# Hybrid block on one core: the tail's order, side work of the attention loop, and the choice of experts from logits

## What is computed

```python
x = x + attn_a(layernorm(x), ...)
x = x + ffn(layernorm(x), Wr, W1, b1, W2, b2)
x = x + attn_b(layernorm(x), ...)
x = x + ffn(layernorm(x), Wr, W1, b1, W2, b2)

def attn_a(x):      # groups of 32 tokens: squared relu attention in the group, and a linear state over earlier groups
    o = (v_quad + v_lin) * gate
    return o @ Wout + bout

def attn_b(x):      # 16 heads of 64; the softmax is over the queries
    scores = einsum('bhqp,bhkp->bhqk', q, k) / sqrt(64)
    ctx = einsum('bhqk,bhkp->bqhp', softmax(scores, axis=2), v)
    return ctx.reshape(b, s, 1024) @ l_w.T + l_b

def ffn(x):         # 8 experts, two for each token, room for 160 tokens an expert and batch
    probs = softmax(x @ Wr); topk_probs, topk_experts = top_k(probs, 2)
    keep = pos < capacity       # pos: place of the token among those of its expert, in order
    h = relu(buf @ W1 + b1); y = h @ W2 + b2
    return (y[of the token's slot] * keep * topk_probs).sum(over the two)
```

## Time and profile before

| | us |
|---|---|
| median of 3 executions (1459.59 to 1462.47) | 1459.8 |
| the profiled execution | 1459.8 |
| its span, first to last instruction | 1458.1 |
| TensorE busy | 1422.4 (98%) |
| VectorE busy | 1071.0 (73%) |
| ScalarE busy | 917.9 (63%) |
| GpSimd busy | 279.9 (19%) |

### The profile page before, as it was taken

One profiled execution on the slowest core, in us unless ns is written; L12 is line 12 of the kernel. 1 busy time (PEld: TensorE's weight loads), 2 busy tenths in 40 slices (PEclk: granted clock), 3 DMA queues, 4 the chain that ended last, 5 costly groups with the idle time before them and its releaser, 6 DMA issues.

```text
span 1458.1 us, 43372 instructions
## 1 busy us (share of the span) xinstructions
PE 1422.4 (98%) x18426; PEld 1016.6 (70%) x18426; DVE 1071.0 (73%) x2172; ACT 917.9 (63%) x1727; POOL 279.9 (19%) x325
## 2 busy tenths in 40 slices
PE   7999989999999999999999999999999999999997
PEld 6989954656777665657777756577777567777487
DVE  6885058898677678886666788876667887787764
ACT  5775756666666666666666666666666666666544
POOL 5165713022210012120000121400000213000046
PEclk9999999999999999999999999999999999999999
DMA  8501311012110111010000110110101111101002
GB/s 224 204 19 56 93 44 43 16 27 53 26 26 17 35 29 31 25 45 17 16 16 17 43 32 22 36 33 17 31 16 40 31 26 33 35 17 31 2 19 59
DMA packets 44464, 58.30 MB, mean 40 GB/s; under 512 B 8231, under 2 KB 32656, under 8 KB 44144
## 3 DMA queue, kind: packets, MB, share of 16 engines
q1 hardware_dynamic: 35120, 38.27, 9.5%
q0 software_dynamic: 9152, 17.26, 4.4%
HBM read 22.14 MB, written 19.32 MB: 28 GB/s over the span
## 4 chain that ended last, share of the span: by engine, by line
PE 87%; DVE 6%; issue 3%; POOL 2%; ACT 2%; DMA 1%; POOLq 0%; DVEq 0%; ACTq 0%
PE bank L1153 30%; PE bank L1166 29%; PE bank L1076 6%; PE bank L1081 4%; PE bank L1090 3%; PE bank L1308 2%; PE bank L1304 2%; PE bank L412 1%; PE bank L1265 1%; PE bank L446 1%; DVE stats L1349 1%; PE bank L830 1%; PE bank L834 1%; PE bank L822 1%; POOL xslots L670 1%
## 5 line engine op out<-in xcount | busy, mean ns | idle before, releaser
L1197 ACT ACTIVATE prob<-bank,nmx 128x1024 f32<-128x1024 f32 x512 | 570.1, 1114 | 396.6 <-DVE nmx L1188 394.6
L1188 DVE TENSOR_REDUCE nmx<-bank 128x1 f32<-128x1024 f32 x512 | 626.7, 1224 | 198.6 <-PE bank L1153 178.0
L1166 PE MATMUL bank<-prob,vsc 64*64 64x512 f32 x4096 | 616.3, 590 | 1.4 <-DVE ctxT L1215 0.7
L1153 PE MATMUL bank<-q,k 64*64 64x512 f32 x2048 | 525.9, 590 | 3.1 <-ACT prob L1197 1.9
L1153 PE MATMUL bank<-q,ks 64*64 64x512 f32 x2048 | 525.6, 590 | 0.0
L1166 PEld LDWEIGHTS bank<-prob,vsc 64*64 64x64 f32 x4096 | 235.8, 133 | 115.1 <-issue 39.4
L1076 PE MATMUL bank<-xT,wqkv_sb 64*64 64x256 f32 (+1 forms) x1560 | 208.6, 434 | 0.0
L1153 PEld LDWEIGHTS bank<-q,ks 64*64 64x64 f32 x2048 | 137.1, 133 | 84.1 <-ACT prob L1197 25.2
L1758 POOL DMA_INDIRECT yg<-yslots,row_ring x64 | 64.7, 1010 | 603.7 <-PE bank L1153 578.2
L1153 PEld LDWEIGHTS bank<-q,k 64*64 64x64 f32 x2048 | 135.7, 133 | 31.5 <-ACT prob L1197 7.9
L1076 PEld LDWEIGHTS bank<-xT,wqkv_sb 64*64 64x64 f32 x1560 | 92.0, 133 | 85.7 <-issue 29.5
(11 more groups left out here) (270 smaller groups left out, 1595.2 us busy)
## 6 DMA issues: line engine op xcount, KB each, us to landing
ks<-k SPq DMA_DIRECT2D x62, 256.0 KB, 3.1
yslots<-slots_sb SPq DMA_DIRECT2D x7, 640.0 KB, 4.0
slots_sb<-xslots SPq DMA_DIRECT2D x5, 640.0 KB, 4.6
xslots<-xhat_r POOLq DMA_DIRECT2D x5, 512.0 KB, 7.1
yslots<-xhat_r POOLq DMA_DIRECT2D x5, 512.0 KB, 12.3
w_sb<-in_w SPq DMA_DIRECT2D x1, 2048.0 KB, 9.5
wqkv_sb<-in_wqkv SPq DMA_DIRECT2D x1, 2048.0 KB, 19.0
xslots<-xhat_r,row_s POOLq DMA_INDIRECT x112
```

Of the source, the lines that this page charges most:

```text
L1153: ins = nc.tensor.matmul(bank[rows(c), SC[h][n], :], kk[r, cols(2 * j + c, HD)], qst[pi % 2][r, cols(n, HALF)], start=True, stop=True)
L1166: ins = nc.tensor.matmul(bank[rows(h), CX[n], :], vsc[s][rows(r), rows(h)], prob[g % 3][h][rows(r), cols(n, HALF)], start=(j == 0 and firs ...
L1188: nc.vector.tensor_reduce(nmx[:, 2 * s + h:2 * s + h + 1], bank[:, SC[h][0]:SC[h][0] + 2, :], mybir.AxisListType.XY, ALU.max, negate=True) ...
L1197: nc.scalar.activation(prob[g % 3][h][:].rearrange("p (n c) -> p n c", c=HALF), bank[:, SC[h][0]:SC[h][0] + 2, :], ACT.Exp, bias=nmx[:, 2 ...
```

## The change

1. **Choice from logits.** `lg` is the logits less their maximum, so the first choice is where it is 0. `first_choice`, `second_choice_begin` and `second_choice_end` find both choices from `lg`; the probabilities come behind, from the exponentials of the two chosen (`chosen_exps`, `chosen_probs`). In the loop the pieces lie in steps 16, 17, 18 and 19 (`F_ROUTE`).
2. **First three batches.** `positions` of the third moves from behind the third expert of m = 1 to ahead of its first. `place_vector` writes the rows itself, the second batch has a buffer of its own (`row_s2`), and each scatter and each of the first gathers has its own event to wait for (`scatter_events`, `gather_events`).
3. **Side work of the loop** by tables: `F_NORM`, `F_NORM_0` for batch 0, `C_NORM`, `COMBINE_FIRST` (one tile a step in place of four in one of four steps). `c_norm_vector` waits for the combines of its batch.
4. **Tail.** Turned slots ahead of the last output product, which now goes to the context's banks; turn of xhat one expert later, logits between an up and a down (`between`); a first tile of the spread ahead of the turned answers, the last two tiles bank by bank (`spread_end_tensor`); the first four of batch 3's answer tiles turned an expert sooner.

```diff
         def choose_vector(v, step, m):
-            v.wait_ge(f_exp, m + 1)
+            v.wait_ge(f_sub, m + 1)
             if m > 1:
                 v.wait_ge(f_idx, m)
-            step.then(nc.vector.tensor_reduce(rsum[:], ex[:], X_AXIS, ALU.add))
-            step.then(nc.vector.reciprocal(rinv[:], rsum[:]))
-            step.then(nc.vector.tensor_tensor(pr[:], ex[:], over_e(rinv[:]), ALU.mult))
-
-            p_now = pr
-            for k in range(2):
-                step.then(nc.vector.tensor_reduce(ptop[:, k, :], p_now[:], X_AXIS, ALU.max))
-                step.then(nc.vector.tensor_tensor(eq[:], p_now[:], over_e(ptop[:, k, :]), ALU.is_equal))
-                step.then(nc.vector.tensor_tensor(key[:], eq[:], rev[:].unsqueeze(1).to_broadcast([P, T, E]), ALU.mult))
-                step.then(nc.vector.tensor_reduce(rk[:], key[:], X_AXIS, ALU.max))
-                step.then(nc.vector.tensor_tensor(oh[:, k], key[:], over_e(rk[:]), ALU.is_equal))
-                if k == 0:
-                    step.then(nc.vector.scalar_tensor_tensor(out=pr2[:], in0=oh[:, 0], scalar=-2.0, in1=pr[:],
-                                                             op0=ALU.mult, op1=ALU.add))
-                    p_now = pr2
+            first_choice(step)
+            second_choice_begin(step)
+            second_choice_end(step)
             nc.vector.tensor_tensor(chosen[:], oh[:, 0], oh[:, 1], ALU.add).then_inc(f_m, 1)
+            v.wait_ge(f_exp, m + 1)
+            chosen_exps(step)
+            chosen_probs(step)
+
+        def first_choice(step):
+
+            step.then(nc.vector.scalar_tensor_tensor(out=key[:], in0=lg[:], scalar=0.0, in1=rev[:].unsqueeze(1).to_broadcast([P, T, E]),
+                                                     op0=ALU.is_equal, op1=ALU.mult))
+            step.then(nc.vector.tensor_reduce(rk[:], key[:], X_AXIS, ALU.max))
+            step.then(nc.vector.tensor_tensor(oh[:, 0], key[:], over_e(rk[:]), ALU.is_equal))
...
+        def chosen_exps(step):
+
+            step.done(nc.vector.tensor_reduce(rsum[:], ex[:], X_AXIS, ALU.add))
+            step.then(nc.vector.tensor_tensor(oh_row[:], oh[:], ex[:].unsqueeze(1).to_broadcast([P, 2, T, E]), ALU.mult))
+            step.done(nc.vector.reciprocal(rinv[:], rsum[:]))
+
+        def chosen_probs(step):
+
+            step.then(nc.vector.tensor_reduce(ptop[:], oh_row[:], X_AXIS, ALU.add))
+            step.then(nc.vector.tensor_tensor(ptop[:], ptop[:], rinv[:].unsqueeze(1).to_broadcast([P, 2, T]), ALU.mult))
...
             step.done(nc.vector.tensor_scalar(skip[:], kept[:], -SKIPPED, SKIPPED, ALU.mult, ALU.add))
             step.then(nc.vector.tensor_tensor(wtok_ring[:, b, :], ptop[:].rearrange("p k t -> p (k t)"),
                                               kept[:].rearrange("p k t -> p (k t)"), ALU.mult))
-            nc.vector.tensor_tensor(skip[:], rowf[:], skip[:], ALU.add).then_inc(f_plc, 1)
+            v.wait_ge(f_sc[1], 256)
+            nc.vector.tensor_tensor(rows_to(m)[:], rowf[:], skip[:], ALU.add).then_inc(f_idx, 1)
 
...
+        def scatter_events():
+
+            r, after = 3, 4
+            second = [None, None, (a_sl, 2 * r + 1), (a_kv, 4 * r + 1), (a_kv, 4 * r + 3), (a_o, 4 * r + 1), (a_o, 4 * r + 2), (lf_tr, 4),
+                      (a_o, 4 * r + 3), (a_o, 4 * r + 4), (f_lg, 3), (a_out, 2 * r + 1), (a_out, 2 * r + 2), (a_xproj, 2 * after + 2),
+                      (a_gproj, 4 * after + 2), (f_pos, 3)]
...
+        def gather_events():
+
+            return [(f_h, 2 * E + 5), (f_y, 2 * E + 3), (f_y, 2 * E + 4), (f_h, 2 * E + 7), (f_h, 2 * E + 8), (f_y, 2 * E + 6), (f_y, 2 * E + 7),
+                    (f_y, 2 * E + 8), (f_h, 3 * E + 1), (f_h, 3 * E + 2), (f_ytr, 8), (f_h, 3 * E + 3), (f_y, 3 * E + 1), (f_h, 3 * E + 4),
+                    (f_y, 3 * E + 2), (f_y, 3 * E + 3)]
...
             c0 = T
             if piece < 2:
+                if b == 1:
+                    v.wait_ge(f_comb, 2 * T * 2 + T + 4 * (piece + 1))
+                elif b == 2:
+                    v.wait_ge(f_comb, 2 * T * 4)
+                elif b == 3:
+                    v.wait_ge(g_comb, 2 * T)
                 stats_vector(v, step, c0, b, range(4 * piece, 4 * piece + 4))
             elif piece == 2:
                 aggr_vector(v, step, c0)
...
-        COMBINE_0 = {5: (1, 0, 0, 4), 6: (1, 0, 4, 8), 14: (1, 1, 0, 4), 15: (1, 1, 4, 8),
-                     43: (2, 0, 0, 4), 46: (2, 0, 4, 8), 52: (2, 1, 0, 4), 55: (2, 1, 4, 8)}
+        COMBINE_FIRST = {1: 6, 2: 42}
+        F_NORM_0 = {2: (0,), 3: (1,), 9: (2,), 10: (3,), 11: (4,), 12: (5,), 13: (6,)}
+        F_NORM = {9: (0, 1), 10: (2, 3), 11: (4,), 12: (5,), 13: (6,)}
+        F_ROUTE = {16: 0, 17: 1, 18: 2, 19: 2.5, 20: 3, 21: 4}
+        C_NORM = {19: (0,), 22: (1,), 25: (2, 3), 26: (4,), 27: (5,), 28: (6,), 33: (7,)}
 
         def side_vector(v, step, g):
             b, s = g // STEPS, g % STEPS
-            if b == 0 and s in COMBINE_0:
-                fb, k, lo, hi = COMBINE_0[s]
-                first_combine_vector(v, step, fb, k, range(lo, hi))
+            for fb, s0 in COMBINE_FIRST.items():
+                if b == 0 and s0 <= s < s0 + 2 * T:
+                    k, t = divmod(s - s0, T)
+                    first_combine_vector(v, step, fb, k, (t,))
...
+            for piece in (F_NORM if b > 0 else F_NORM_0).get(s, ()):
+                f_norm_vector(v, step, b, piece)
+            if s in F_ROUTE:
+                f_route_vector(v, step, b, F_ROUTE[s])
+            if b < B - 1 and s in C_NORM:
+                for piece in C_NORM[s]:
+                    c_norm_vector(v, step, b + 1, piece)
...
                         for t in range(whole):
                             ins = pj_piece(g, 1, False, t)
                         ins.then_inc(pj_done(g), 1)
-            pe.wait_ge(c_res, 2 * (NPAIRS - 1))
+            pe.wait_ge(c_exp, 2 * (LAST + 1))
+            slots_tensor(pe, B, slots_sb, TR[:2] + [(0, *TR[2][1:])])
+            for n in range(2):
+                out_tensor(pe, NPAIRS - 1, n, CX[n])
             pe.wait_ge(g_free, len(CHUNK))
-            for n in range(2):
-                out_tensor(pe, NPAIRS - 1, n, PJ[n])
-            slots_tensor(pe, B, slots_sb, TR[:2] + [(0, *TR[2][1:])])
 
...
         def last_experts_scalar(a, m):
             def beside(e):
-                if e == E - 1:
-                    answers_scalar(a, m, range(2))
+                if e >= E - 2 and e < E:
+                    answers_scalar(a, m, [e - E + 2])
...
         def last_experts_tensor(pe, m):
 
             def beside(e):
-                if e == E - 1:
-                    pe.wait_ge(f_ya, E * m + E - 2)
-                    for n in range(2):
-                        answers_turn_tensor(pe, n)
+                if e >= E - 2 and e < E:
+                    pe.wait_ge(f_ya, E * m + (4, E - 2)[e - E + 2])
...
-        def spread_tensor(pe, m):
+        def spread_piece(pe, t, bk, lo, hi):
+            for part in (xh_hi, xh_lo):
+                ins = nc.tensor.matmul(bank[:, bk, 0:(hi - lo) * P], part[:, t, :], oh_t[t][:, lo * P:hi * P],
+                                       start=(t == 0 and part is xh_hi), stop=(t == T - 1 and part is xh_lo))
+            return ins
+
+        def spread_tensor(pe, tiles):
             pe.wait_ge(t_lo, 2)
-            for t in range(T):
+            for t in tiles:
                 pe.wait_ge(t_oh, t + 1)
                 for bk, lo, hi in SPREAD:
-                    for part in (xh_hi, xh_lo):
-                        ins = nc.tensor.matmul(bank[:, bk, 0:(hi - lo) * P], part[:, t, :],
-                                               oh_t[t][:, lo * P:hi * P],
-                                               start=(t == 0 and part is xh_hi), stop=(t == T - 1 and part is xh_lo))
-                    if t == T - 1:
-                        ins.then_inc(f_str, 1)
+                    spread_piece(pe, t, bk, lo, hi)
+
+        def spread_end_tensor(pe, tiles):
+            pe.wait_ge(t_oh, T)
+            for bk, lo, hi in SPREAD:
+                for t in tiles:
+                    ins = spread_piece(pe, t, bk, lo, hi)
+                ins.then_inc(f_str, 1)
 
         def last_norm_tensor(pe):
             def beside(e):
-                if e == 2:
+                if e == 3:
                     route_turn_tensor(pe, B - 1, LN_ROUTE)
...
+                if e == E:
+                    spread_tensor(pe, range(1))
             return beside
+
+        def last_logits_tensor(pe):
+            def between(e):
+                if e == 4:
+                    logits_tensor(pe, B - 1, LN_ROUTE)
+            return between
...
```

155 lines of the change are left out of this document (63 added, 92 removed).

## The result

The changed kernel takes 1449.7 us, median of 4 executions (1448.68 to 1450.68), against 1459.69 for the kernel before (4 executions, 1459.45 to 1462.47). The ratio is 0.993, interval 0.9918 to 0.9941: faster by 10.0 us. The forecast was 1451.2 in a range of 1447.5 to 1455.5. The profiled execution took 1448.82, with a span of 1447.1 (1458.1 before), so the traces differ by 11.0 us, one more than the medians.

The account below looks back on a forecast made before the run. TensorE was taken to bound the loop (80% of the span) and GpSimd's 32 indirect DMAs the end. Gains of 2.5 (front), 3.7 (loop) and 2.4 (tail) sum to 8.6: 1459.8 - 8.6 = 1451.2 us, range 1447.5 to 1455.5.

Parts of the forecast that it names:

- Choice: Choice from logits: two rows of attention a gain 0.33 us each; in the loop, steps 18 and 19 gain 1.5.
- Scatters: Front: the third batch's scatters follow right on the second's, so its slots load sooner; gain 0.65 us.
- Gathers: Front: batch one's gathers end sooner, so TensorE's 2.36 us gap ahead of the turned xhat shrinks by 0.85.
- Step 24: Loop: moving statistics out of step 23 brings step 24 to 4.52 us, 0.47 less in three batches, 1.4.
- Step 8: Loop: step 8 keeps 0.1 to 0.23 of its 0.47 us; gain 0.9 in three batches, 0.8 in batch 0.
- Combines: Loop, batch 0: combines one at a time in place of four gain 0.2 us.
- Packing: Loop: closer-packed side work on VectorE costs 0.1 us in each of six places, and 0.3 for batch 0.
- The tail: Behind the loop: first up 1.7 us sooner, row_s 1.6, GpSimd's thirteenth issue and the end 2.4.
- Rival 1: The loop gives nothing: VectorE's backlog costs 0.5 us a place and takes back 3.7; 1454.9 us, chance 0.15.
- Rival 2: Only TensorE moves in the tail; GpSimd's issues stretch or wait, front gathers too; 1453 us, chance 0.10.
- Rival 3: The stalls were all one backlog and vanish whole, the 2.36 gap too; 11.5 gained, 1448.3 us, chance 0.11.
- Rival 4: Slower: batch 0's sixteen single combines each wait out a GpSimd DMA issue; 11 us lost, 1462.2, chance 0.04.

Follow-up runs that it names:

- p_meet: Changed kernel with GpSimd's bias addition of the second batch held for ScalarE's second xT_hi of the same row; 1470.08 us, ratio 0.9909 to the kernel before.
- r_loop_back: Changed kernel with that bias addition ahead of the zeroing wait and VectorE's side work of the loop as before; 1453.79 us, ratio 0.9955.
- r_best: Changed kernel with the early addition, first norm's statistics spread over steps 8 and 9, its later pieces shifted, batch 0's combines one step earlier; 1448.69 us, ratio 0.9924.
- the q runs: Changed kernel with the early addition, alone or with the old front, old tail order or old choice; 1469.37, 1479.42, 1471.30 and 1476.18 us.
- p_before: Kernel before with GpSimd's bias addition of the second batch moved ahead of its wait for the zeroing DMAs; 1482.98 us, ratio 0.9992.
- q_tail_back: Changed kernel with the early addition and the tail's order of the kernel before, choice from logits kept; 1471.30 us, ratio 0.9912.

## The prediction against the runs

**What bounds it** was right. The tail is GpSimd's chain from row_s on, and TensorE's lead there is worth nothing of its own.

**The front**: forecast 2.5, found 3.0, and 1.4 more that is none of the change. *Choice*: 0.35 for two rows less lock and product time, found 0.65 up to 130 us. The step that was mis-sized is "the whole block ends about 0.33 sooner": the block ends 0.58 sooner (the residual moves from 72.75 to 70.79, 1.38 of it from the meeting at 40 us), and 0.09 of that goes to a longer wait for the positions behind the residual (0.24 in place of 0.15). The lock at row 3 is real: GpSimd's small products took 0.66 and 0.76 in place of 0.32 and VectorE's lkT 0.98 in place of 0.81, which took back 0.5 at 110 us, 0.2 of it only until 113, not the 0.15 that was set aside. The Trainium skill (SBUF — State Buffer, "SBUF: two separate sides") has the two engines lock a shared port pair for a whole instruction, whichever starts first. The rows at 40 us and in p_meet bear out the lock. Who gets it can't be told there from the recorded starts: in p_meet the addition stood 0.48 ahead of the second xT_lo and still waited for it. *Positions*: 0.5 forecast, 0.61 net. *Scatters*: 0.65 forecast, 0.83. *Gathers*: 0.85 forecast, 0.86; the gap ahead of xhat is 1.50.

**The loop**: forecast 3.7, found 4.3. Step 24: 1.4 forecast, 1.63 (0.69 in batch 0). Step 8: 0.9 + 0.8 forecast, 1.40 + 0.51; what was to be left of it, "between 0.1 and 0.23 of its 0.47", was nothing in batches 1 to 3. Combines: 0.2 forecast, 0.40, the second half in step 56, which the prediction had not looked at. Choice: 1.5 forecast, 1.08; 0.22 in step 18 and 0.05 in step 19, where the rest of 19's length was TensorE's own work read as a stall. Packing: 0.6 + 0.3 set aside, 0.36 + 0.31 found (r_loop_back and r_best show both as backlog).

**The tail**: 2.4 forecast, 2.4 found. The steps hold one by one (first up 1.64 of 1.7, row_s 1.60 of 1.6, thirteenth issue 2.36 of 2.4), but one cause is other than told: the thirteenth issue moved "because that event moves by 2.6"; the event came early enough for the wait to vanish, and GpSimd's own 1.60 and the lost 0.77 of waiting make the 2.36. By this reading a still earlier event would have left the end where it is, which no run tested. And the sum 0.6 + 0.3 + 0.7 for row_s is not made of three separate gifts: the q runs show that order without choice costs 0.4 and choice without order gives 0.3.

**Rivals.** Rival 1 fell: packed statistics and Newton parts cost 0.05 to 0.10 a place. Rival 2 fell: GpSimd's issues moved as forecast (the last gather 2.4). Rival 3 (every stall whole, 11.5) is near for the loop and wrong for the xhat gap, which is still 1.50. The median alone does not choose: 1449.7 lies 1.5 below the forecast and 1.4 above rival 3's 1448.3. Rival 4 fell: sixteen single combines in batch 0 cost 0.31 in steps 21 to 23 and nothing elsewhere.

## What to carry to other kernels

A short instruction group costs nothing in a step with room, and a good part of its length (here 0.47 of 0.86 us) where what the next step needs first is queued behind it: look for what stands behind side work, not for how much there is. A new order and a shorter dependence can be worth more together than one by one, so undo each alone before crediting either. Where two engines share a port and one starts on a DMA's landing, one trace shows one of two outcomes: compare starts ahead of the first changed line before giving a difference to the change.

## What was not expected of the hardware

- Two executions of the same instructions differed by 2.2 us on VectorE (1.26 and 3.44 for two 128x512 subtractions with both inputs in SBUF), by whether a 128x1024 addition of GpSimd started 0.39 or 0.55 us behind the first of them; at 0.10 behind, it was the addition that waited.
- The point at which TensorE's first matmuls go from 0.43 to 0.23 us apart lay between 15.8 us (p_before) and past 17.6 us (q_tail_back) from the start, and moved everything behind it by up to 1.4 us.
- With 2.1 us idle in 5, TensorE was granted 1.2 GHz for part of the next 3 us in one trace of the old front (1.96 us gap) and stayed at 2.4 GHz in another (2.36 us gap, 2.2 idle in 5); in four traces with 1.50 it stayed.
- In eight runs ScalarE stood idle, up to 9.5 us at a time, with no releaser in the profile, and all kernels alike were 20 to 25 us longer. What it waited for is open.
